# A prologue, a first chunk and a last step in another order, in a fused attention and feed-forward kernel on one core

## The chip, the core and the metric

The kernel runs as one program on one core of a Trainium2 chip. The core has five engines, each with its own list of instructions: PE (TensorE, matmuls and transposes into PSUM), DVE (VectorE), ACT (ScalarE), POOL (GpSimd) and SP (SyncE, which here only issues transfers). They meet through semaphores. Weights are loaded into PE by instructions of their own (PEld). PSUM has eight banks of 128 x 512 f32.

The metric is the device time of one execution in microseconds (us). Three runs of the kernel before took 366.59, 364.92 and 367.21 us, with a median of 366.59.

## What is computed

128 sequences of 64 tokens with 128 features (8192 tokens), all in f32:

```
x = x + xattn(ctx, ctx, layernorm(x))            # 16 heads of 8 features
x = x + ffn(layernorm(x))

xattn: k = KEY @ Wk.T + bk ; v = VALUE @ Wv.T + bv ; q = QUERY @ Wq.T + bq
       score[b,h,i,k] = k[b,h,i] . q[b,h,k] / sqrt(8)
       attn = softmax(score, axis=1)             # axis 1: over the heads
       out  = attn * v, heads joined, @ Wo.T + bo
ffn:   h = x; for blk in 0, 1, 2:
           y = qlora_linear(h; 2 blk); y = gelu(layernorm(y) * gamma + beta)
           y = qlora_linear(y; 2 blk + 1); h = y + h
qlora_linear: w = (q / 7.5 - 1) * scale (one for 16 inputs); x @ w.T + bias + (x @ la.T) @ lb.T
```

## The kernel before, in words

**Attention.** The tokens go through in 16 chunks of 512. Chunk c is worked in four parts p = 0 to 3, each of two sequences. For a part, PE computes the scores of 16 heads into one of two score tiles (`scores`, L1356), DVE takes the maximum over the heads (`negmax`, L815), PE adds its negative with two bf16 matmuls (L1495), ACT takes the exponential (`exponentials`, L1108), DVE sums over the heads and inverts (`zsum` L829, `rz` L832), POOL multiplies (`probs`, L518), and PE multiplies with v, laid out in blocks in `v_diag` (L1564). Between these, the queries and keys of chunk c+2 are made: transposes of the context (L1368) and of the normalised input (L1374), projections (L1380 for q, L1386 for k), and the split of each result in two f16 parts (`q_high`, `q_low`, `k_high`, `k_low` on ACT, with a matmul for the remainder between them, L1400 and L1406). The parts are stored to DRAM by SP and gathered back into `q_stack` and `k_stack` in the layout of the scores. v is projected for chunk c+1 (L1393). DVE also takes the moments of the input three chunks ahead (L607).

**Order.** Nothing is scheduled by a tool: each engine's list is the order in which its function calls stand in `prologue`, `chunk(c, par, half)`, `step(t, par)` and `last_steps`. An engine works strictly down its list, so a wait holds up all that stands behind it on the same engine. `chunks` writes out chunks 0, 1 and 12 to 17 one by one and loops over 2 to 11. Work that is done once stands in the chunks under a condition on (c, p).

**Prologue and work done once.** The prologue loads the first inputs and the weights, makes the queries of chunk 0 in two halves (`first_q_part`), and its keys (`first_key_parts`, DVE, L696 and L699). `keep_awake(n)` is n matmuls of the identity whose result nobody reads. The feed-forward weights are made once: `dequantised_weights` (DVE), `low_rank_products` (PE, six matmuls, L1309), `effective_weights` (DVE: w_eff as their sum, and a fold of the mean into the first, L725 to L738), `transpose_layers` (PE, L1320 and L1321), `transposed_layers` (ACT copies them to `lin_t`, L966), and `first_layer_rows` (PE) with `first_layer_seeds` (DVE, L743 to L753), which make two rows that start later accumulations. In before, `low_rank_products` and the first v projection (`project_v(0)`, into the tile `work0`) stand in part (0, 0) of PE, `effective_weights` in part (0, 1) of DVE after rz, `transpose_layers` in (0, 2) and (1, 0), `first_layer_rows` in (1, 1) and the seeds in (1, 2).

**Feed-forward.** From chunk 13 on and after the attention, `step(t, par)` runs the three blocks as a pipeline over chunks: first layer, moments on DVE, the inverse deviation on POOL (`rs`, a power, L565), scaling on ACT (`normalise`, L1187), transposes on PE, gelu on ACT, second layer. `last_steps` finishes chunks 13 to 15 of the third block; chunk 15 is done in halves of 256 tokens. There, `residual_rows` and `last_layer` put the output of one chunk after the other into the same bank 6, and DVE adds it to x (`add_output`, L921, and L944 for the halves), after which SP stores it.

## Time and profile before

| | |
|---|---|
| median of three runs | 366.59 us (364.92 to 367.21) |
| profiled execution | 366.99 us |
| its span, first to last instruction | 365.0 us |
| PE busy | 342.1 us, 94% |
| DVE busy | 329.3 us, 90% |
| ACT busy | 289.4 us, 79% |
| POOL busy | 267.6 us, 73% |
| mean granted clock of TensorE | 0.986 of 2.4 GHz |

The profiled execution took 2.0 us more than its span; that part lies outside of the instructions. A share of busy time is a mean over stages with different limits. Timeline rows give start and duration in us, then engine, line, operation, tile written and tiles read; a time in square brackets is how long the engine stood idle before the row, with what released it. Consecutive instructions of one engine overlap by 0.1 to 0.2 us in these rows, so the distance between two starts is less than a duration.

### The profile page before, as it was taken

How to read it: one execution, taken by the hardware profiler on the slowest of the kernel's cores; microseconds unless marked ns; L12 is line 12 of the kernel's file. 1: busy time of each engine (PE TensorE's matmuls, PEld its weight loads, DVE VectorE, ACT ScalarE, POOL GpSimd, SP SyncE). 2: the span in 40 equal slices, each digit the busy share in tenths (PEclk: the TensorE clock that was granted, in tenths of full speed). 3: DMA queues.
4: the chain of work that ended last, by engine and by line, in shares of the span. 5: the costliest groups of instructions: out<-in, count | busy, mean ns of one | idle time of the engine just before them, and what ended most of it. 6: DMA issues, size and time to landing. Idle time of an engine off the chain costs nothing.

```text
span 365.0 us, 13072 instructions
## 1 busy us (share of the span) xinstructions
PE 342.1 (94%) x4797; PEld 255.7 (70%) x4797; DVE 329.3 (90%) x816; ACT 289.4 (79%) x587; POOL 267.6 (73%) x287
## 2 busy tenths in 40 slices
PE   6778999999999999999999798988999999999985
PEld 5454666667667667766766576865888888888874
DVE  5798999999999999999999989979999999988762
ACT  4567888888788878878887757668889999999973
POOL 4456688789878877987897998878877788774231
PEclk9889999999999999999999989999999999999999
DMA  7794566576458547645843400000010001101112
GB/s 196 204 284 131 181 203 200 147 237 199 146 172 251 166 135 224 202 155 160 259 137 128 145 2 4 2 1 3 14 47 29 29 29 41 48 30 31 57 31 87
DMA packets 54514, 43.29 MB, mean 119 GB/s; under 512 B 4608, under 2 KB 48592, under 8 KB 54480
## 3 DMA queue, kind: packets, MB, share of 16 engines
q1 hardware_dynamic: 53904, 42.31, 38.5%
q10 hardware_dynamic: 576, 0.53, 0.5%
q8 instruction: 21, 0.34, 0.4%
q14 instruction: 13, 0.11, 0.1%
HBM read 26.05 MB, written 16.78 MB: 117 GB/s over the span
## 4 chain that ended last, share of the span: by engine, by line
PE 64%; DVE 17%; POOL 6%; ACT 6%; issue 5%; DMA 1%; DVEq 0%; ACTq 0%; POOLq 0%
PE score_ps L1594 9%; PE att_ps L1564 6%; PE score_ps L1495 6%; PE wo_ps L1344 5%; DVE zsum L829 4%; PE score_ps L1356 4%; DVE negmax L815 4%; PE score_ps L1687 3%; PE work L1680 3%; PE work L1380 3%; POOL probs L518 3%; PE work L1393 3%; PE work L1386 3%; PE att_ps L1687 3%; PE score_ps L1588 2%
## 5 line engine op out<-in xcount | busy, mean ns | idle before, releaser
L518 POOL TENSOR_TENSOR probs<-probs,rz 128x1024 f32<-128x1024 f32 x64 | 136.3, 2139 | 33.6 <-DVE rz L832 33.5
L565 POOL TENSOR_TENSOR rs<-ve,minus_half 128x4 f32<-128x4 f32 (+1 forms) x48 | 56.6, 1181 | 37.9 <-DVE ve L765 28.4
L829 DVE TENSOR_REDUCE zsum<-probs 128x64 f32<-128x1024 f32 x64 | 77.3, 1209 | 2.2 <-ACT probs L1108 2.0
L815 DVE TENSOR_REDUCE negmax<-score_ps 128x64 bf16<-128x1024 f32 x64 | 75.4, 1180 | 2.0 <-PE score_ps L1356 2.0
L1108 ACT ACTIVATE probs<-score_ps 128x1024 f32<-128x1024 f32 x64 | 65.6, 1025 | 14.2 <-PE score_ps L1495 13.7
L1344 PEld LDWEIGHTS wo_ps<-wo_t,att_t 128*128 128x128 f32 x256 | 37.0, 192 | 13.6 <-issue 12.2
L1564 PE MATMUL att_ps<-probs,v_diag 128*32 128x64 f32 x2048 | 43.8, 225 | 1.3 <-POOL probs L518 1.3
L1594 PEld LDWEIGHTS score_ps<-lin_t,h 128*128 128x128 f32 x304 | 36.9, 191 | 11.1 <-DVE h L914 7.0
L1187 ACT ACTIVATE z<-score_ps,rs 128x128 f32<-128x128 f32 x152 | 43.5, 382 | 0.3 <-POOL rs L565 0.3
L1495 PE MATMUL score_ps<-negmax,ident_bf 128*128 128x512 bf16 x128 | 39.1, 387 | 3.0 <-DVE negmax L815 3.0
L1594 PE MATMUL score_ps<-lin_t,h 128*128 128x128 f32 x304 | 39.7, 278 | 1.8 <-DVE h L914 1.8
L1564 PEld LDWEIGHTS att_ps<-probs,v_diag 128*32 128x32 f32 x2048 | 33.1, 109 | 11.0 <-issue 2.4
L1344 PE MATMUL wo_ps<-wo_t,att_t 128*128 128x128 f32 x256 | 38.1, 275 | 0.0
L832 DVE RECIPROCAL rz<-zsum 128x64 f32<-128x64 f32 x64 | 35.4, 553 | 2.2
L861 DVE BATCH_NORM_STATS2 st<-score_ps 128x6 f32<-128x128 f32 x152 | 33.8, 285 | 3.3 <-PE score_ps L1594 2.2
L1356 PE MATMUL score_ps<-q_stack,k_stack 64*64 64x128 f16 x1024 | 26.8, 223 | 1.5 <-DMA k_stack<-k_parts 0.6
L1356 PEld LDWEIGHTS score_ps<-q_stack,k_stack 64*64 64x64 f16 x1024 | 16.8, 106 | 13.1 <-issue 11.1
L468 POOL TENSOR_TENSOR half_rstd<-veps,minus_half 128x4 f32<-128x4 f32 x16 | 16.3, 1017 | 11.4 <-DVE veps L619 10.4
L1027 ACT ACTIVATE v_diag<-work 64x512 f32<-64x512 f32 x32 | 18.8, 586 | 2.9 <-PE work L1393 2.6
L975 ACT ACTIVATE xln<-x_all,half_rstd 128x128 f32 (+1 forms) x60 | 19.1, 392 | 0.5 <-POOL half_rstd L468 0.5
L1393 PEld LDWEIGHTS work<-w_t_v,ctx_tr 128*128 128x128 f32 x128 | 17.6, 199 | 2.2
L1198 ACT ACTIVATE g<-score_ps,cols 128x512 f32<-128x512 f32 x21 | 16.8, 799 | 2.7 <-PE score_ps L1588 2.7
(234 smaller groups left out, 687.4 us busy)
## 6 DMA issues: line engine op xcount, KB each, us to landing
q_parts<-parts SPq DMA_DIRECT2D x15, 512.0 KB, 3.5
k_stack<-k_parts SPq DMA_DIRECT2D x30, 256.0 KB, 3.3
q_stack<-q_parts SPq DMA_DIRECT2D x60, 128.0 KB, 3.0
ctx_sb<-in_ctx SPq DMA_DIRECT2D x16, 256.0 KB, 3.7
k_parts<-parts SPq DMA_DIRECT2D x16, 256.0 KB, 2.8
out<-x_all SPq DMA_DIRECT2D x15, 256.0 KB, 2.3
x_all<-in_x SPq DMA_DIRECT2D x14, 256.0 KB, 3.9
x_all<-in_x SPq DMA_DIRECT2D x1, 512.0 KB, 5.5
```

What stands on the lines that cost most here:

```text
L518: nc.gpsimd.tensor_tensor(e[:, :, :, :], e[:, :, :, :], by_query.broadcast_to([P, BANDS, SEQ, ADJ]), ALU.mult).then_inc(s_probs, 1)
L565: nc.gpsimd.tensor_tensor(rs2[v][:, lo:hi], ve2[v][:, lo:hi], minus_half[:, lo:hi], ALU.pow).then_inc(p_rs[v], 1)
L815: nc.vector.tensor_reduce(negmax[p % 2][:, :], score_ps[p % 2][:, :].rearrange("p (h k) -> p k h", k=SEQ), AX_X, ALU.max, negate=True).the ...
L829: nc.vector.tensor_reduce(zsum[q][:, :], probs[(p - 1) % 4][:, :, :, :].rearrange("p u k s -> p k u s"), AX_XY, ALU.add).then_inc(s_zsum, 1)
L832: nc.vector.reciprocal(rz[(p - 1) % 4][:, :], zsum[q][:, :]).then_inc(s_rz, 1)
L1108: nc.scalar.activation(probs[p][:, :, :, :], score_ps[p % 2][:, :].rearrange("p (u s k) -> p u k s", s=ADJ, k=SEQ), ACT.Exp, scale=SCALE). ...
L1187: ins = nc.scalar.activation(z[v][0][:, t, :], src[:, TILE * t:TILE * (t + 1)], ACT.Copy, scale=rs2[v][:, lo + t:lo + t + 1])
L1344: ins = nc.tensor.matmul(wo_ps[:, TILE * t:TILE * (t + 1)], att[:, o, TILE * u:TILE * (u + 1)], wo_t[:, o, b, :], start=False, stop=o == 1 ...
L1356: ins = nc.tensor.matmul(score_ps[mp % 2][SEQ * b:SEQ * (b + 1), c0:c0 + 2 * SEQ], k_stack[mb][half_rows, grp, k0:k0 + SEQ], q_stack[mb][h ...
L1495: ins = nc.tensor.matmul(score_ps[p % 2][:, CHUNK * o:CHUNK * (o + 1)], ident_bf[:, :], negmax[p % 2][:, :].unsqueeze(1).broadcast_to([P, ...
L1564: ins = nc.tensor.matmul(att_ps[32 * grp:32 * (grp + 1), c0:c0 + SEQ], v_diag[mb][:, v0:v0 + 32], probs[mp][:, band(hd), :, hd % ADJ], sta ...
L1594: ins = nc.tensor.matmul(dst[:, TILE * t:TILE * (t + 1)], hk[:, TILE * t:TILE * (t + 1)], lin_t[:, 2 * v - 2, :], start=v == 1 and t == 0, ...
```

## The change

Three places are edited.

**The prologue and chunks 0 and 1.** SP loads chunk 2 of x ahead of the weights, the context of chunk 2 ahead of the first stores, and chunk 3 of x alone after the first gathers (before, chunks 2 and 3 came in one transfer after the weights). DVE takes the moments of chunk 1 before the first key parts and those of chunk 2 right behind them. POOL clears the second q_stack before the inverse deviation of chunk 1. PE gets three more `keep_awake` matmuls, `low_rank_products` in two parts in the prologue, and ACT another order of the same copies. In the chunks, v of chunk 0 goes to `wo_ps` instead of `work0` and is projected before the shift of part 0; the transposed layers get two banks, and come in (0, 1) and (0, 2) instead of (0, 2) and (1, 0); the rows come in (0, 3) and the seeds in (1, 0); `effective_weights` stands ahead of zsum in (0, 1). ACT copies the value blocks in (0, 1) instead of (0, 0), and the transposed layers between the high and the low parts.

**The last steps.** Chunk 15's first layer of the third block uses banks 1 and 7, seeded early; its moments, powers and scalings are done by halves, the second scaling by DVE; outputs 14 and 15 have banks of their own (0, 4 and 2) instead of bank 6 in turn.

```diff
@@ sync, prologue
+                sp.dma_start(x_all[:, 2, :, :], x_t[2]).then_inc(s_xin[2], 16)
                 for k, src in (("v", wv), ("o", wo)):
...
-                sp.dma_start(x_all[:, 2:4, :, :], x_pt[:, 2:4, :, :]).then_inc(s_xin[2], 16)
+                sp.wait_ge(s_ctx_ps, 1)
+                sp.dma_start(ctx_sb[0][:, :, :], ctx_t[2]).then_inc(s_ctxin[0], 16)
...
                 gather_first_q(1, s_stack[0])
-                sp.wait_ge(s_ctx_ps, 1)
-                sp.dma_start(ctx_sb[0][:, :, :], ctx_t[2]).then_inc(s_ctxin[0], 16)
+                sp.dma_start(x_all[:, 3, :, :], x_t[3]).then_inc(s_xin[3], 16)
@@ gpsimd, prologue
+                clear(q_stack[1][:, :, :, :].bitcast(F32).rearrange("p g s t -> p (g s t)"), s_const)
                 first_scale(1)
-                clear(q_stack[1][:, :, :, :].bitcast(F32).rearrange("p g s t -> p (g s t)"), s_const)
@@ vector, prologue and chunk
                 bias_columns()
+                next_input(1)
                 first_key_parts()
-                next_input(1)
+                next_input(2)
                 output_weights()
+                low_rank_rows()
                 bias_parts()
-                low_rank_rows()
                 dequantised_weights()
-                next_input(2)
+                last_effective_weights()
...
+                        else:
+                            dve.wait_ge(s_xin[3], 16)
                         dve.wait_ge(s_rstd, c + 3)
                         input_stats_of(c + 3)
+                    if isinstance(c, int) and (c, p) == (0, 1):
+                        effective_weights()
...
-                    if isinstance(c, int) and (c, p) == (0, 1):
-                        effective_weights()
-                    if isinstance(c, int) and (c, p) == (1, 2):
+                    if isinstance(c, int) and (c, p) == (1, 0):
                         first_layer_seeds()
@@ scalar, chunk 0
                     q_high(c + 2, par)
+                    if isinstance(c, int) and c == 0:
+                        transposed_layers(0)
                     q_low(c + 2, par)
+                if isinstance(c, int) and c == 0:
+                    act.wait_ge(s_v_ps, 1)
+                    act.wait_ge(s_vzero, 2)
+                    value_blocks(0, 0, wo_ps)
@@ tensor, prologue
                 transpose_context(0)
+                keep_awake(1)
                 pe.wait_ge(s_wq, 3)
                 nc.tensor.transpose(bank[0][:, 0:P], wq_c[:, :], ident[:, :]).then_inc(s_tr, 1)
+                keep_awake(2)
                 first_transposes(0, wo_ps, h_xln, h_xln_ps)
...
                 project_k(1, 1)
+                low_rank_products(0)
                 project_q(1)
                 k_remainder(1, 1)
+                low_rank_products(1)
                 q_remainder(1, 1)
@@ vector, last steps
                 for u in range(2):
+                    st, ag = st2[3][:, 2 * u:2 * u + 2, :], ag2[3][:, :, 2 * u:2 * u + 2]
                     dve.wait_ge(l_y3, u + 1)
...
+                add_output(13, bank[6])
+                dve.wait_ge(l_rs, 2)
+                dve.wait_ge(l_zt[2], 2)
+                for i in range(2):
+                    ins = nc.vector.tensor_scalar(z[2][0][:, 2 + i, :], last_first_layer(1)[:, TILE * i:TILE * (i + 1)],
+                                                  rs2[3][:, 2 + i:3 + i], None, ALU.mult)
+                ins.then_inc(l_zh, 1)
+                add_output(14, bank[0])
```

The lists show it at three places. First PE, from the scores of parts 0 and 1 on. `work` stands for the tiles work0 and work1, `q_stack` and `score_ps` for both of their buffers. Before:

```order
L1356 MATMUL score_ps<-q_stack,k_stack 64x128 [waits s_lbt,h_stack,h_k_stack]
L1356 MATMUL score_ps<-q_stack,k_stack 64x128 x31
L1495 MATMUL score_ps<-negmax,ident_bf 128x512 [waits s_negmax]
L1495 MATMUL score_ps<-negmax,ident_bf 128x512
L1309 MATMUL att_ps<-la_in,lb_t 128x128 [waits h_q_lo,s_wready,s_lbt]
L1309 MATMUL att_ps<-la_in,lb_t 128x128 x3
L1309 MATMUL wo_ps<-la_in,lb_t 128x128 x2
L1328 MATMUL work<-bias_h,pick_row 128x512 [waits s_q_lo,s_split,s_pick]
L1393 MATMUL work<-w_t_v,ctx_tr 128x128 x4
L1368 MATMUL work<-ident,ctx_sb 128x2x64 [waits s_k_lo,s_ctxin0]
L1368 MATMUL work<-ident,ctx_sb 128x2x64 x3
L1374 MATMUL work<-ident,xln 128x128 [waits s_v,s_xln]
```

And now:

```order
L1391 MATMUL score_ps<-q_stack,k_stack 64x128 [waits h_stack,h_k_stack]
L1391 MATMUL score_ps<-q_stack,k_stack 64x128 x15
L1391 MATMUL score_ps<-q_stack,k_stack 64x128 [waits s_wready]
L1391 MATMUL score_ps<-q_stack,k_stack 64x128 x15
L1363 MATMUL wo_ps<-bias_h,pick_row 128x512 [waits s_split,s_pick,s_weff]
L1428 MATMUL wo_ps<-w_t_v,ctx_tr 128x128 x4
L1541 MATMUL score_ps<-negmax,ident_bf 128x512 [waits s_negmax]
L1541 MATMUL score_ps<-negmax,ident_bf 128x512
L1403 MATMUL work<-ident,ctx_sb 128x2x64 [waits s_k_lo,s_ctxin0]
L1403 MATMUL work<-ident,ctx_sb 128x2x64 x3
L1409 MATMUL work<-ident,xln 128x128 [waits s_q_lo,s_xln]
```

The v projection moved ahead of the shift and into another tile, the low-rank products left this place, and the transposes of the next input no longer wait for the value blocks (s_v).

Second DVE, from the third reciprocal `rz` of chunk 0 to the maximum of part (1, 1). Now:

```order
L829 TENSOR_REDUCE negmax<-score_ps 128x64 [waits s_shifted,s_scores]
L847 TENSOR_REDUCE zsum<-probs 128x64 [waits s_exp]
L850 RECIPROCAL rz<-zsum 128x64 [waits s_zsum]
L756 TENSOR_SCALAR res_cols<-cols 128x1
L757 TENSOR_TENSOR res_cols<-cols 128x1
L761 TENSOR_REDUCE seed_sum<-wo_ps 128x2 [waits s_seed_ps]
L763 TENSOR_SCALAR seed_mean<-seed_sum 128x2 [waits s_seed]
L766 TENSOR_SCALAR seed<-wo_ps,seed_mean 128x128 [waits s_seed]
L766 TENSOR_SCALAR seed<-wo_ps,seed_mean 128x128
L829 TENSOR_REDUCE negmax<-score_ps 128x64 [waits s_shifted,s_scores]
```

The six instructions of the seeds stood six parts' operations later, behind the reciprocal of part (1, 1); they are now right behind that of part (0, 3).

Third ACT at the end. Before:

```order
L1240 ACTIVATE g<-score_ps,cols 128x512 [waits p_c3,p_zt3]
L1267 ACTIVATE z_0<-score_ps,rs_3 128x128 [waits p_rs3]
L1267 ACTIVATE z_0<-score_ps,rs_3 128x128 x3
L1240 ACTIVATE g<-score_ps,cols 128x256 [waits l_zt3,p_c3]
L1240 ACTIVATE g<-att_ps,cols 128x256 [waits l_zt3]
```

And now:

```order
L1297 ACTIVATE z_0<-score_ps,rs_3 128x128 [waits l_rs]
L1297 ACTIVATE z_0<-score_ps,rs_3 128x128
L1274 ACTIVATE g<-score_ps,cols 128x512 [waits p_c3,p_zt3]
L1274 ACTIVATE g<-score_ps,cols 128x256 [waits l_zt3,p_c3]
L1274 ACTIVATE g<-wo_ps,cols 128x256 [waits l_zt3]
```

Two of the four scalings of chunk 15 moved ahead of the gelu of chunk 14, and two left ACT.

## Rows read from the trace of the kernel before

**Rows 1.** Waits of 50 to 190 us: us in total, times, longest us.
```profile
DVE zsum L829 <- ACT probs L1108: 0.4, 2, 0.2
```

**Rows 2.** Chain of waits: start, us, what.
```profile
16.09 4.71 DMA k_stack<-k_parts
...
21.14 0.44 PE score_ps L1356 x16
```

**Rows 3.** Windows: length, busy us of PE, PEld, DVE, ACT, POOL, granted clock, DMA share, GB/s.
```profile
8.20:11.50 3.30, 3.30 (x7) 1.62 (x7) 0.75 (x1) 1.27 (x6) 0.00 (x0) 0.50 1.17 248
```

**Rows 4.** Timeline of PE: the same key projection at either clock.
```profile
8.08 2.07 PE L1386 MATMUL work<-ctx_tr,w_t_k 128*128 128x512 f32 x2
...
17.42 1.12 PE L1386 MATMUL work<-ctx_tr,w_t_k 128*128 128x512 f32 x2 [0.16 <-ACT ctx_tr L983]
```

**Rows 5.** Timeline of DVE in the prologue.
```profile
11.80 0.75 DVE L699 TENSOR_SCALAR parts<-work,cols_h 128x512 f16<-128x512 f32 x1 [0.78 <-PE work L1406]
12.47 0.86 DVE L607 BATCH_NORM_STATS2 stats<-x_all 128x6 f32<-128x128 f32 x4
```

**Rows 6.** Timeline of SP's queue: key store, query gathers.
```profile
13.05 0.61 SPq L363 DMA_DIRECT2D k_parts<-parts  x1
...
15.49 3.91 SPq L391 DMA_DIRECT2D q_stack<-q_parts  x8
```

**Rows 7.** Timeline of DVE in chunks 0 and 1.
```profile
21.61 2.36 DVE L815 TENSOR_REDUCE negmax<-score_ps 128x64 bf16<-128x1024 f32 x2 [0.71 <-PE score_ps L1356]
...
26.91 0.41 DVE L727 TENSOR_TENSOR w_eff<-wo_ps,w_deq 128x256 f32<-128x256 f32 x1
...
27.55 1.13 DVE L733 TENSOR_TENSOR fold<-cols,fold 128x1 f32<-128x1 f32 x1
...
29.55 1.22 DVE L815 TENSOR_REDUCE negmax<-score_ps 128x64 bf16<-128x1024 f32 x1 [0.36 <-PE score_ps L1356]
31.13 1.22 DVE L829 TENSOR_REDUCE zsum<-probs 128x64 f32<-128x1024 f32 x1 [0.35 <-ACT probs L1108]
...
36.11 1.23 DVE L815 TENSOR_REDUCE negmax<-score_ps 128x64 bf16<-128x1024 f32 x1 [0.20 <-PE score_ps L1356]
37.87 1.22 DVE L829 TENSOR_REDUCE zsum<-probs 128x64 f32<-128x1024 f32 x1 [0.53 <-ACT probs L1108]
...
39.59 1.16 DVE L815 TENSOR_REDUCE negmax<-score_ps 128x64 bf16<-128x1024 f32 x1
...
45.94 0.10 DVE L743 TENSOR_SCALAR res_cols<-cols 128x1 f32<-128x1 f32 x1
```

**Rows 8.** Timeline of POOL beside it.
```profile
26.53 2.13 POOL L518 TENSOR_TENSOR probs<-probs,rz 128x1024 f32<-128x1024 f32 x1 [2.67 <-DVE rz L832]
...
29.88 1.01 POOL L468 TENSOR_TENSOR half_rstd<-veps,minus_half 128x4 f32<-128x4 f32 x1
```

**Rows 9.** Timeline of DVE: two casts, before and after POOL began to clear.
```profile
14.98 0.22 DVE L663 CAST bias<-row_r 16x128 bf16<-16x128 f32 x1
...
15.22 0.52 DVE L664 CAST row_mid<-row_r 16x128 bf16<-16x128 f32 x1
```

**Rows 10.** Timeline of POOL beside them.
```profile
15.12 2.10 POOL L494 MEMSET q_stack<- 128x512 f32 x4
```

**Rows 11.** Timeline of ACT in the last steps.
```profile
356.86 0.78 ACT L1240 ACTIVATE g<-score_ps,cols 128x512 f32<-128x512 f32 x1 [1.30 <-PE score_ps L1588]
358.57 1.14 ACT L1267 ACTIVATE z<-score_ps,rs 128x128 f32<-128x128 f32 x4 [0.93 <-POOL rs L565]
360.39 0.56 ACT L1240 ACTIVATE g<-score_ps,cols 128x256 f32<-128x256 f32 x1 [0.68 <-PE score_ps L1694]
```

**Rows 12.** Timeline of PE in the last steps.
```profile
357.69 1.16 PE L1705 MATMUL work<-lin_t,g 128*128 128x128 f32 x8 [0.43 <-ACT g L1240]
```

**Rows 13.** Timeline of DVE: the last addition.
```profile
362.21 0.42 DVE L944 TENSOR_TENSOR x_all<-score_ps,x_all 128x256 f32<-128x256 f32 x1
```

**Rows 14.** The page, DMA issues: count, KB each, median us to landing.
```profile
x_all<-in_x SPq DMA_DIRECT2D x14, 256.0 KB, 3.9
```

More of the change, by code:

```diff
@@ L195, in build @@
         s_seed = sem("s_seed")
-        s_xin = [sem(f"s_xin{i}") for i in range(3)]
+        s_xin = [sem(f"s_xin{i}") for i in range(4)]
         s_xnext = [sem(f"s_xnext{i}") for i in range(2)]
@@ L309, in turned_bank, with last_first_layer @@
         def turned_bank(i):
[L311 removed]
+            return (att_ps if i < 4 else wo_ps)[:, P * (i % 4):P * (i % 4 + 1)]
+        def last_first_layer(u):
+            return (bank[1], bank[7])[u][:, 0:2 * TILE]
         def half_tiles(u):
@@ L598, in _ @@
             steps(pool, step)
-            for t in (20, 21):
-                step(t, t % 2)
+            step(20, 0)
+            pool.wait_ge(p_z[3], 15)
+            for u in range(2):
+                pool.wait_ge(l_st, u + 1)
+                nc.gpsimd.tensor_tensor(rs2[3][:, 2 * u:2 * u + 2], ve2[3][:, 2 * u:2 * u + 2],
+                                        minus_half[:, 2 * u:2 * u + 2], ALU.pow).then_inc(l_rs, 1)
         @block.vector
@@ L1093, in prologue @@
                 q_low(1, 1)
-                transposed("v", bank[5], 4)
-                act.wait_ge(s_tr, 5)
-                nc.scalar.activation(wo_t[:, :, :, :].rearrange("p o b n -> p (o b n)"), bank[4],
-                                     ACT.Copy).then_inc(s_wready, 1)
                 nc.scalar.activation(neg_last[:, :], cols[:, ROW_BL + 5:ROW_BL + 6].broadcast_to([P, P]), ACT.Copy,
@@ L1254, in last_steps @@
                 gelu(3, g[2][:, :], bank[3])
-                act.wait_ge(p_z[2], 16)
-                half_seed(0)
                 normalise(3, 14, 0, 15, bank[0])
-                act.wait_ge(p_z[3], 15)
-                half_seed(1)
+                act.wait_ge(l_rs, 1)
+                for t in range(2):
+                    ins = nc.scalar.activation(z[2][0][:, t, :], last_first_layer(0)[:, TILE * t:TILE * (t + 1)], ACT.Copy,
+                                               scale=rs2[3][:, t:t + 1])
+                ins.then_inc(l_z[3], 1)
                 act.wait_ge(p_zt[3], 15)
@@ L1263, in last_steps @@
                 gelu(3, g[2][:, :], bank[3])
-                act.wait_ge(p_rs[3], 16)
-                for t in range(TPC):
-                    u = t // 2
-                    ins = nc.scalar.activation(z[3][0][:, t, :], bank[1 - u][:, TILE * t:TILE * (t + 1)], ACT.Copy,
-                                               scale=rs2[3][:, t:t + 1])
-                    if t == 1:
-                        ins.then_inc(l_z[3], 1)
-                ins.then_inc(p_z[3], 1)
                 act.wait_ge(p_c[3], 15)
@@ L1275, in last_steps @@
                     act.wait_ge(l_zt[3], u + 1)
-                    gelu(3, g[2][:, half_columns(u)], bank[(3, 4)[u]][:, half_columns(u)])
+                    gelu(3, g[2][:, half_columns(u)], bank[(3, 5)[u]][:, half_columns(u)])
             prologue()
@@ L1517, in chunk @@
                         project_q(c + 2)
+                    if isinstance(c, int) and (c, p) == (0, 1):
+                        transpose_layers(0)
                     if p == 2 and live(c + 2):
@@ L1707, in last_layer @@
                     return ins
+                pe.wait_ge(p_h[0], 16)
+                nc.tensor.matmul(last_first_layer(1), ident_bf[:, :], pick_row[:, 0:2, :], start=True,
+                                 stop=True).then_inc(l_open, 1)
                 pe.wait_ge(p_h[2], 15)
```

165 lines of the change are left out of this document (89 added, 76 removed).

## The prediction

> **What bounds the kernel now.** I read the busy shares first: PE 94% and DVE 90% both look like the bound, so shares don't decide. The waits of the steady loop do. Between 50 and 190 us DVE waited 0.4 us in all [rows 1]: there it is the bound, with PE close behind, and nothing in this change touches the loop. So a lead that DVE has when it enters the loop is a lead at the end of the loop, and a microsecond that PE alone wins is worth nothing. What is left is the start, up to about 47 us, and the last 15 us.
>
> At the start the chain of waits runs through the first gathers of the keys: the second one is issued at 16.09, lands 4.71 later, and the scores begin at 21.14 [rows 2]. Ahead of it TensorE works at half its clock: granted 0.50 (1.2 GHz) from 8.2 to 11.5 us, after a stretch with three gaps of 0.4 to 0.5 us in which it waited for a context, a weight and an input [rows 3]. The same key projection takes 2.07 us there and 1.12 us at the full clock [rows 4]. Behind the first scores I read DVE's timeline: from its first maximum to the fourth reciprocal it has five stretches in which it does no work of its own [rows 7].
>
> **The prologue.** The three added keep_awake matmuls fill 0.2 and 0.45 us of those gaps and end before the wait behind them is over, so they delay nothing. I take it that the clock then stays up. That is worth at least 0.95 us (the projection alone, 2.07 - 1.12) and at most 1.65 us (half of 3.3 us at half clock [rows 3]). Step by step: the projection starts at 8.08 as now and ends at 9.2, the first key part takes 0.75 (as L699 [rows 5]), the remainder 0.45, so the second key part starts at 10.4 instead of 11.80 [rows 5]: 1.4 us. The moments of chunk 1, at 12.47 now [rows 5], go into the time in which DVE waits for the key projection, and the inverse deviation of chunk 1 is no longer what the scalings and, behind them on ACT, the key gathers stand in line for. The key store then goes out at 11.7 (now 13.05), and the query gathers at 13.7 (now 15.49 [rows 6]), since the two stores between them come off a shorter chain. The gathers' bytes are the same, so I let the 4.7 us of [rows 2] run from 1.4 to 1.8 us earlier: scores at 19.5 instead of 21.14, **1.65 us**. What is added there is hidden: the low-rank products on PE stand in the wait for the gathers (the last matmul of the prologue ends near 18.4 by the same steps); the last effective weights on DVE end near 19.4, just before the first maximum at 19.95. That margin of 0.5 us is thin, and I charge nothing for it.
>
> **Chunk 0.** From 21.61 to 39.59 DVE takes 17.98 us for four maxima pairs, one set of moments, the effective weights and four sums with reciprocals [rows 7]. Of these, 0.36 + 0.35 + 0.20 + 0.53 = 1.44 us are waits for PE and ACT. Another 0.97 us is one instruction, the fold on one column: 1.13 us where its like takes 0.16. It ends at 28.68, and POOL's multiplication, 26.53 + 2.13, at 28.66 [rows 7, 8]: a DVE instruction with two inputs in SBUF is held until POOL's is over. In the new order it runs near 23.8, when POOL has nothing to do before the first reciprocal (26.4), so this goes. A third piece, 0.32 us of L727 [rows 7], moves to the prologue. Do the waits go? PE's list up to the scores of part 2 loses the low-rank products and the wait for the value blocks: these scores come at 23.0 (DVE wants them at 26.3), those of part 3 at 26.0 (wanted 29.2), part (1, 0) at 30.2 (wanted 32.0), the third exponential ends at 29.2 (wanted 30.3). The least slack is 0.8 us, so DVE works without a gap. 1.44 + 0.97 + 0.32 = **2.73 us**. Below it would be 1.3 (no wait goes), above nothing.
>
> **The seeds.** They are moved, so their 1.3 us of work costs the same. But their place is new: right behind the reciprocal of part 3, at 35.2. POOL is late there: multiplication 0 ends at 28.6, the variance of the input, which ends with the power at 29.88 + 1.01 [rows 8], holds it until 30.9, and multiplications 1, 2 and 3 follow without a gap until 33.0, 35.15 and 37.3. L757 of the new list is the same operation with the same form as the fold, two inputs in SBUF, one column. If it or the seed mean behind it is held until multiplication 3 ends, DVE loses 2.1 us; if both pass in the handover at 35.15, nothing. For the mean, with one input, the rows are further off: a cast took 0.22 us just before POOL began to clear at 15.12 and 0.52 us after it [rows 9, 10], so one input from SBUF to SBUF can be held too. I take **2.0 us lost**, by the fold, which is nearest.
>
> The Trainium skill (SBUF — State Buffer, Who interferes with whom) says that VectorE and GpSimd share a pair of ports with an exclusive lock, taken by a VectorE instruction with two SBUF inputs while GpSimd reads, and by a tensor_scalar that gets into a two-port mode. By it the seed mean is held even if L757 slips through, which speaks against this change; the loss would be 2.0 us in either order. The row of the fold agrees with the first half; no row of before shows the second for a tensor_scalar.
>
> Start of the loop: 1.65 + 2.73 - 2.0 = **2.4 us** earlier on DVE, and kept to the end of the loop.
>
> **The last steps.** Now the gelu of chunk 14 ends at 357.64, its last layer at 358.85, and from then on the buffer g is free for the halves of chunk 15, yet their gelu starts at 360.39: 1.54 us [rows 11, 12]. In between stand four scalings (1.14 us, behind the gelu), the addition that frees bank 6, and two transposes. With half of the scalings ahead of the gelu, the other half on DVE and banks of their own, nothing is left in this gap but the semaphore, 0.04. The first two scalings (0.6 us) fall in the 1.30 us in which ACT waits for this gelu's input [rows 11], but come late in it, and one opening matmul is added on PE: together the gelu starts 0.2 later. **1.3 us**; the second half's power and DVE's scaling end near 358.0, 0.7 before they are wanted, so the new wait hides. Bounds: 0 (the halves' chain just replaces the old one) to 1.5. From the gelu's start to the last addition, 360.39 to 362.63 [rows 11, 13], all stays.
>
> **Sum.** 366.99 - 2.4 - 1.3 = 363.3 us for the profiled execution. It stood 0.4 above the median, so I forecast **362.9 us**.
>
> **Rivals.**
> - *The seeds are not held.* For it: the loss hangs on POOL's being three multiplications behind, and the handover at 35.15 lies 0.05 us from where the seeds start. Against it: the fold. Time 360.9.
> - *The clock falls all the same,* or falls in another place as costly. For it: the gap before the context, 0.5 us, stays, and the granted clock fell a second time, at 25 us, after a busier stretch. Then the 1.65 us are not won: 364.5.
> - *The end gives nothing:* 364.2. For it: six waits among four engines are new there. Against it: each is early by my times.
> - *Slower, by the load of chunk 3.* DVE now waits for it at 22.3 before the effective weights, the first sum and the first reciprocal, with PE's transposed layers and the scores of part 3 queued behind. It goes out at 17.5, after eight gathers, and such a load takes 3.9 us [rows 14], so it lands at 21.4, with 0.9 to spare. Every microsecond after 22.3 costs one; from 26.0 on the kernel is slower than before, and at 27.0 it takes 367.6. Nothing in the profile shows a load of 9.5 us.
>
> **Chances.** The forecast 0.48, the seeds not held 0.24, the clock 0.15, nothing at the end 0.09, the load 0.04. 1% is 3.7 us, about what a measurement of this kernel can tell from no change: below 362.9 counts as faster. My forecast lies on that line; a little over half of it I give to faster. With the seeds not held, all of it is faster; the next two are within 1%. So faster 0.51, within 1% 0.45, slower 0.04. The range of 360.7 to 365.0 takes in the first four cases with their own spread and leaves out what lies below the second and the slow one.
>
> **What would show it.** The granted clock from 8 to 11.5 us at 1.00 and the key projection at 1.1 us; the first scores near 19.5; the fold at 0.16 us near 24; DVE without waits from its first maximum to the fourth reciprocal; L757 or L763 lasting 1 to 2 us, ending with a POOL multiplication; DVE 2.4 us ahead when it is in the loop (the maximum that stood at 47.2 after the seeds); no gap between the last layer of chunk 14 and the gelu of chunk 15. I am wrong if DVE waits for the scores or exponentials of chunk 0, or if its lead shrinks inside the loop, which would mean that PE or a transfer is the bound there.

## The result: 0.9% faster, and the profile after

The changed kernel takes 362.09 us (median of 15 runs, 361.35 to 363.73), the one before 365.87 us (15 runs, 362.86 to 368.21). The ratio is 0.9914, 95% interval 0.9886 to 0.9941 (the two medians alone give 0.990). Ratios in this text leave out runs more than 1.5% above the fastest of their kernel; medians keep them. The forecast was 362.9 us. The profiled execution of the change took 362.27 us with a span of 360.4, against 366.99 and 365.0 before: 4.6 us of span, where the sum had 3.7.

The first thing that differs is TensorE's clock. The page of the profile shows it in slices of 9 us, each digit the granted clock in tenths; before and after:

```profile
PEclk9889999999999999999999989999999999999999
```

```profile
PEclk9999899999999999999999999999999999999999
```

Before, the granted clock fell at 8, at 25 and at 209 us; after, once, at 39 us, and neither at 8 nor at 25. The windows of after show the stretch of [rows 3], then the two microseconds before the fall, and the fall itself (columns as there):

```profile
8.20:11.50 3.30, 2.76 (x11) 1.39 (x10) 2.11 (x8) 2.33 (x9) 3.12 (x7) 1.00 1.09 220
36.90:39.00 2.10, 0.13 (x9) 0.07 (x2) 2.06 (x6) 0.35 (x1) 0.18 (x1) 1.00 0.68 221
39.30:42.70 3.40, 3.40 (x37) 1.44 (x35) 3.37 (x6) 1.71 (x2) 1.26 (x1) 0.51 0.03 8
```

Between 36.9 and 39.0 TensorE worked for 0.13 us in all. DVE's timeline says what it waited for. These rows answer to [rows 7]:

```profile
19.87 2.35 DVE L829 TENSOR_REDUCE negmax<-score_ps 128x64 bf16<-128x1024 f32 x2
...
23.95 0.16 DVE L746 TENSOR_TENSOR fold<-cols,fold 128x1 f32<-128x1 f32 x1
...
26.25 1.16 DVE L829 TENSOR_REDUCE negmax<-score_ps 128x64 bf16<-128x1024 f32 x1
...
31.82 1.16 DVE L829 TENSOR_REDUCE negmax<-score_ps 128x64 bf16<-128x1024 f32 x1
...
34.14 0.55 DVE L850 RECIPROCAL rz<-zsum 128x64 f32<-128x64 f32 x1
34.61 0.10 DVE L756 TENSOR_SCALAR res_cols<-cols 128x1 f32<-128x1 f32 x1
34.62 0.37 DVE L757 TENSOR_TENSOR res_cols<-cols 128x1 f32<-128x1 f32 x1
34.91 0.41 DVE L761 TENSOR_REDUCE seed_sum<-wo_ps 128x2 f32<-128x256 f32 x1
35.35 1.75 DVE L763 TENSOR_SCALAR seed_mean<-seed_sum 128x2 f32<-128x2 f32 x1
37.14 0.61 DVE L766 TENSOR_SCALAR seed<-wo_ps,seed_mean 128x128 f32<-128x128 f32 x2
37.66 1.21 DVE L829 TENSOR_REDUCE negmax<-score_ps 128x64 bf16<-128x1024 f32 x1
```

From the first maximum to that of part (1, 0) no row has an idle time in brackets. The fold takes 0.16 us where it took 1.13. Then the seed mean takes 1.75 us where it took 0.17 in its old place. POOL beside it, and the matmul that waits for the late maximum:

```profile
30.74 6.33 POOL L524 TENSOR_TENSOR probs<-probs,rz 128x1024 f32<-128x1024 f32 x3
```

```profile
38.94 0.81 PE L1541 MATMUL score_ps<-negmax,ident_bf 128*128 128x512 bf16 x2 [1.97 <-DVE negmax L829]
```

POOL's three multiplications end at 37.07, the seed mean at 37.10. TensorE waits 1.97 us for the next maximum.

At the end ACT shows the other part of the change; the rows answer to [rows 11]:

```profile
353.50 0.78 ACT L1274 ACTIVATE g<-score_ps,cols 128x512 f32<-128x512 f32 x1
355.81 0.56 ACT L1274 ACTIVATE g<-score_ps,cols 128x256 f32<-128x256 f32 x1 [1.53 <-PE score_ps L1737]
```

From the gelu of chunk 14 (ends 354.28) to the first of chunk 15 there are now 1.53 us; before there were 2.75 (357.64 to 360.39).

How far DVE is at the same maxima, from its timelines, in us. Two more executions stand beside the two: one of either kernel in which the clock never fell (the runs "before again" and "after again" below), and the changed kernel with its seeds in the old place.

| DVE is at | before | after | before, clock up | after, clock up | seeds back |
|---|---|---|---|---|---|
| maximum (0, 0) | 21.61 | 19.87 | 19.87 | 20.13 | 19.77 |
| maximum (1, 0) | 36.11 | 31.82 | 33.47 | 32.08 | 31.71 |
| maximum (1, 1) | 39.59 | 37.66 | 36.95 | 37.93 | 34.50 |
| maximum (1, 3) | 47.20 | 44.06 | 44.55 | 44.33 | 42.11 |
| maximum (3, 0) | 62.51 | 59.93 | 59.85 | 59.57 | 57.41 |
| maximum (5, 2) | 93.94 | 91.73 | 91.33 | 91.41 | 88.84 |
| maximum (13, 2) | 195.19 | 193.03 | 192.58 | 192.73 | 190.15 |
| maximum (15, 0) | 216.51 | 213.13 | 212.66 | 212.84 | 210.23 |
| last addition | 362.21 | 357.63 | 358.30 | 357.41 | 354.74 |

The first two columns are the pair that was forecast: 1.74 us ahead at the first maximum, 4.29 at (1, 0), 3.14 behind the seeds, 2.16 in the loop, 3.38 behind the fall at 209, 4.58 at the end. The third and fifth are what the rest of this text is about: with the clock up, the first maximum of the kernel before stands at 19.87 too.

### The profile page after: what moved, and what is told of

Same layout as the page of the kernel before. It is cut to its first block, busy times and chain, and to the rows that moved or that the text cites. A ratio compares the mean times of both kernels' runs of the same rounds, so it can differ in the third digit from the quotient of the medians.

```text
span 360.4 us, 13093 instructions
## 1 busy us (share of the span) xinstructions
PE 340.1 (94%) x4804; PEld 254.6 (71%) x4804; DVE 331.7 (92%) x821; ACT 288.2 (80%) x585; POOL 266.8 (74%) x288
## 4 chain that ended last, share of the span: by engine, by line
PE 62%; DVE 23%; POOL 5%; issue 5%; ACT 3%; DVEq 0%; POOLq 0%; ACTq 0%
PE score_ps L1637 9%; PE att_ps L1600 7%; DVE zsum L847 6%; PE score_ps L1541 5%; DVE negmax L829 5%; PE wo_ps L1379 5%; PE score_ps L1391 3%; PE score_ps L1730 3%; PE work L1723 3%; PE work L1415 3%; POOL probs L524 3%; PE att_ps L1730 3%; PE score_ps L1631 2%; PE work L1428 2%; PE work L1421 2%
## 5 line engine op out<-in xcount | busy, mean ns | idle before, releaser
L524 POOL TENSOR_TENSOR probs<-probs,rz 128x1024 f32<-128x1024 f32 x64 | 136.2, 2141 | 37.0 <-DVE rz L850 36.9
L571 POOL TENSOR_TENSOR rs<-ve,minus_half 128x4 f32<-128x4 f32 (+1 forms) x47 | 55.6, 1184 | 34.3 <-DVE ve L778 24.7
L1379 PEld LDWEIGHTS wo_ps<-wo_t,att_t 128*128 128x128 f32 x256 | 36.9, 191 | 13.4 <-issue 12.0
L1637 PEld LDWEIGHTS score_ps<-lin_t,h 128*128 128x128 f32 x304 | 36.9, 191 | 11.1 <-DVE h L930 7.0
L1723 PEld LDWEIGHTS work<-lin_t,g 128*128 128x128 f32 x104 | 13.7, 192 | 6.2 <-issue 6.2
L1058 ACT ACTIVATE v_diag<-work 64x512 f32<-64x512 f32 x30 | 17.6, 585 | 0.3
```

Of the source, the lines that this page charges most:

```text
L524: nc.gpsimd.tensor_tensor(e[:, :, :, :], e[:, :, :, :], by_query.broadcast_to([P, BANDS, SEQ, ADJ]), ALU.mult).then_inc(s_probs, 1)
L571: nc.gpsimd.tensor_tensor(rs2[v][:, lo:hi], ve2[v][:, lo:hi], minus_half[:, lo:hi], ALU.pow).then_inc(p_rs[v], 1)
L1379: ins = nc.tensor.matmul(wo_ps[:, TILE * t:TILE * (t + 1)], att[:, o, TILE * u:TILE * (u + 1)], wo_t[:, o, b, :], start=False, stop=o == 1 ...
L1637: ins = nc.tensor.matmul(dst[:, TILE * t:TILE * (t + 1)], hk[:, TILE * t:TILE * (t + 1)], lin_t[:, 2 * v - 2, :], start=v == 1 and t == 0, ...
```

## Experiments

There were four series, each on another chip and beside its own runs of the kernel before: experiments 1 to 4, 5 to 7, 8 to 11, and 12. The ratio is to these runs. One more run of the kernel before, in the first series, took 836.88 us at a mean clock of 1.0; it is left out everywhere. "Clock up" counts the runs whose mean granted clock was 0.998 or more; every fall of some 3.5 us takes 0.005 off that mean. Of the kernel before 4 of 33, 0 of 11, 2 of 16 and 1 of 11 runs kept the clock up in the four series, so counts from different series are compared with care.

| kernel | runs | median us | ratio, 95% | clock up | their median | mean clock |
|---|---|---|---|---|---|---|
| before, beside the experiments | 71 | 365.78 | | 7 | 363.31 | 0.990 |
| after | 15 | 362.09 | 0.9914 (0.9886 to 0.9941) | 7 | 361.49 | 0.9955 |
| keep_awake only | 12 | 366.34 | 1.0013 (0.9976 to 1.0050) | 3 | 363.73 | 0.989 |
| after, no keep_awake | 12 | 362.83 | 0.9936 (0.9906 to 0.9965) | 4 | 362.09 | 0.994 |
| start only | 12 | 363.76 | 0.9941 (0.9914 to 0.9968) | 6 | 363.51 | 0.9965 |
| end only | 11 | 363.93 | 0.9945 (0.9908 to 0.9983) | 2 | 361.92 | 0.992 |
| seeds back | 6 | 360.28 | 0.9842 (0.9796 to 0.9887) | 5 | 359.95 | 0.998 |
| no mean | 6 | 360.00 | 0.9841 (0.9794 to 0.9888) | 5 | 359.86 | 0.9985 |
| seeds and fold back | 11 | 363.60 | 0.9919 (0.9887 to 0.9951) | 0 | | 0.9885 |
| seeds back, no keep_awake | 6 | 361.30 | 0.9871 (0.9832 to 0.9911) | 0 | | 0.993 |
| seeds back, no mean | 6 | 359.17 | 0.9814 (0.9776 to 0.9852) | 6 | 359.18 | 0.9997 |
| the same, rank later | 6 | 360.23 | 0.9853 (0.9805 to 0.9901) | 3 | 359.63 | 0.995 |

### 1. The three matmuls alone

```diff
                 transpose_context(0)
+                keep_awake(1)
                 pe.wait_ge(s_wq, 3)
...
+                keep_awake(2)
                 first_transposes(0, wo_ps, h_xln, h_xln_ps)
```

> The kernel before with nothing but the three added keep_awake matmuls. Theory (the clock's fall at 8.2 us comes from TensorE's gaps before it, and the time to the scores hangs on the key projection): granted clock 1.00 from 8 to 11.5 us, key projection 1.1 instead of 2.07, first maximum at 20.0 to 20.7 instead of 21.61, time 0.9 to 1.6 us below the kernel before. Rival (the matmuls are too few, or the scores wait for the deviation and the gathers of chunk 1's neighbours, not for the projection): clock 0.5 there again or the first maximum within 0.3 of 21.61, time within 0.4 us.

The profile has the clock up from 8 to 11.5 us and the first maximum at 20.31, 1.3 us earlier than in the profile of before: that half of the theory holds. The time does not follow: 366.34 us, no difference that can be measured. The profiled execution is one of the long ones, because the clock fell later instead:

```profile
22.80:36.50 13.70, 12.40 (x72) 8.31 (x71) 9.31 (x17) 6.31 (x9) 6.19 (x8) 0.50 0.39 125
```

13.7 us at the lower level, and DVE 2.9 us behind the profile of before at (1, 1). Five of the 12 runs had a mean clock of 0.984 or less, against 7 of 33 of the kernel before in that series. So filling the first gaps kept the clock up at 8 us in this profile, and did not keep later falls away while chunk 0 is as before.

### 2. The change without them

```diff
                 transpose_context(0)
-                keep_awake(1)
...
-                keep_awake(2)
                 first_transposes(0, wo_ps, h_xln, h_xln_ps)
```

> The changed kernel without the three added keep_awake matmuls. Theory: the clock falls at 8 us again, the key projection takes 2 us, the first maximum comes 0.9 to 1.7 us later than 19.87, and the time rises by the same, to 0.9 to 1.7 above the changed kernel. Rival (the new order alone has closed the gaps): the clock stays up without them, the first maximum at 19.9, no difference over 0.3 us.

The clock fell at 8 us in the profile, and the first maximum stands at 21.09, 1.22 later than 19.87. But the median rises by 0.7 only, and 4 of 12 runs kept the clock up. These 0.7 us are not clear of noise (the two intervals overlap, and the runs come from different series), and with the clock up the two still differ by 0.6 (362.09 against 361.49), so how much of it is falls is not shown. Part of the lost lead came back further on: that profile had no fall at 39 us, and at (3, 0) it is 0.6 behind the changed kernel.

### 3 and 4. The start alone, the end alone

Start only is the changed kernel with the last steps as before; end only the reverse. In DVE's list of the latter:

```diff
-                add_output(13)
 
                 for u in range(2):
+                    st, ag = st2[3][:, 2 * u:2 * u + 2, :], ag2[3][:, :, 2 * u:2 * u + 2]
                     dve.wait_ge(l_y3, u + 1)
...
+                add_output(13, bank[6])
+                dve.wait_ge(l_rs, 2)
+                dve.wait_ge(l_zt[2], 2)
```

> The changed kernel with the last steps of the kernel before. Theory (the two halves of the change add up, and the end gives the 1.2 us by which ACT's gap before the last gelus shrank): 1.2 us above the changed kernel, gelu gap 2.75 us again. Rival (the end was shortened by an earlier arrival of work that is off the path): under 0.5 us above.

> The kernel before with the last steps of the changed kernel. Theory: 1.2 us below the kernel before, gap on ACT between the gelu of chunk 14 and the first of chunk 15 1.5 us instead of 2.75; nothing changes ahead of 340 us, and the three falls of the granted clock stay where they were. Rival: under 0.5 us below.

Taking the end away costs 1.7 us (363.76 against 362.09, from different series), giving it alone wins 1.6 (363.93 against 365.54 in that series). The profiles put it in one gap on ACT. Start only, and end only:

```profile
357.43 0.56 ACT L1253 ACTIVATE g<-score_ps,cols 128x256 f32<-128x256 f32 x1 [0.67 <-PE score_ps L1719]
```

```profile
355.49 0.78 ACT L1265 ACTIVATE g<-score_ps,cols 128x512 f32<-128x512 f32 x1
357.79 0.56 ACT L1265 ACTIVATE g<-score_ps,cols 128x256 f32<-128x256 f32 x1 [1.53 <-PE score_ps L1716]
```

The second has the gap of 1.53 us again. So the end is worth 1.2 us of gap, and 0.4 more in the medians, which the profiles don't place.

One part of the expectation missed, and it opened the case: end only has the prologue of before, word for word, yet its first maximum stands at 20.13 and the clock did not fall at 8. Falls belong to the run, not to the kernel alone. And of the start, with the clock up, hardly anything is left: 363.51 us against 363.31 for the kernel before.

### 5 to 7. The seeds, and the kernel before once more

Seeds back:

```diff
-                    if isinstance(c, int) and (c, p) == (1, 0):
+                    if isinstance(c, int) and (c, p) == (1, 2):
                         first_layer_seeds()
```

No mean (the seeds stay at (1, 0)):

```diff
-                nc.vector.tensor_scalar(seed_mean[:, :], seed_sum[:, :], -1.0 / D, None, ALU.mult).then_inc(s_seed, 1)
-                dve.wait_ge(s_seed, 3)
                 for v in range(2):
-                    ins = nc.vector.tensor_scalar(seed[:, v, :], raw[:, v, :], seed_mean[:, v:v + 1], None, ALU.add)
+                    ins = nc.vector.scalar_tensor_tensor(seed[:, v, :], seed_sum[:, v:v + 1].broadcast_to([P, P]),
+                                                         -1.0 / D, raw[:, v, :], ALU.mult, ALU.add)
```

> The changed kernel with the first layer's seeds back in their old place, behind part (1, 2). Theory (the seeds were held in the new place until POOL's multiplications ended, which starved TensorE for 2 us and brought the clock down at 39 us): the seed mean takes 0.17 us instead of 1.75, the maximum of part (1, 1) stands near 35.3 instead of 37.66, that of part (1, 3) near 42.4 instead of 44.06, no gap of 2 us on PE near 37 and no fall of the clock at 39; time 0.8 to 1.6 us below the changed kernel. Rival (TensorE is the next bound, so DVE's lead is taken back in the first chunks of the loop): the same at part (1, 3), but DVE waits for exponentials from then on and the time is within 0.5 us of the changed kernel.

> The changed kernel with the seeds in their new place, but the seed mean (tensor_scalar from SBUF to SBUF) taken out: the sum goes straight into a scalar_tensor_tensor that reads one operand in SBUF and one in PSUM. Theory (it is this instruction's form that is held by POOL): no instruction of the seeds lasts over 0.7 us, maximum of part (1, 1) near 35.9 instead of 37.66. Rival (whatever follows the reciprocal there is held): the hold of 1.6 us moves to the next instruction and part (1, 1) stays near 37.6. Time: as with the seeds in the old place, within 0.4 us, by the first; as the changed kernel by the second.

> The kernel before once more, for one profile in which the granted clock may fall less often than in the first (33 runs of it spread from 363.1 to 369.4 us with their mean clock between 1.0 and 0.981). With fewer falls the first maximum should stand near 20.1 (as in the run with only the end changed) instead of 21.61.

Both are 1.8 to 2.1 us below the changed kernel, a little more than the 0.8 to 1.6 that I had expected. Seeds back:

```profile
34.50 1.16 DVE L829 TENSOR_REDUCE negmax<-score_ps 128x64 bf16<-128x1024 f32 x1
...
41.38 0.17 DVE L763 TENSOR_SCALAR seed_mean<-seed_sum 128x2 f32<-128x2 f32 x1
```

No mean, with POOL beside it:

```profile
35.12 0.38 DVE L757 TENSOR_TENSOR res_cols<-cols 128x1 f32<-128x1 f32 x1
35.42 0.41 DVE L761 TENSOR_REDUCE seed_sum<-wo_ps 128x2 f32<-128x256 f32 x1
35.87 0.48 DVE L764 SCALAR_TENSOR_TENSOR seed<-seed_sum,wo_ps 128x128 f32<-128x128 f32 x2
36.27 1.22 DVE L828 TENSOR_REDUCE negmax<-score_ps 128x64 bf16<-128x1024 f32 x1
```

```profile
31.25 6.34 POOL L524 TENSOR_TENSOR probs<-probs,rz 128x1024 f32<-128x1024 f32 x3
```

POOL multiplies until 37.59, and four instructions of DVE pass beside it: one operand in SBUF and one in PSUM is not held, nor is a reduction. L757, with both in SBUF, is held for 0.23 us, up to the handover between two multiplications. So the first theory of each holds: it is the seed mean, a `tensor_scalar` of 128x2 from SBUF to SBUF, that was held for 1.58 us. One input from SBUF to SBUF is not enough for a hold. The rows of the changed kernel above have two such instructions beside the same multiplications, and neither is held: the reciprocal at 34.14 (0.55 us, as everywhere else) and L756 at 34.61, a `tensor_scalar` of one column (0.10 us). The rival of seeds back (the lead is taken back in the loop) falls: DVE is 2.45 us ahead of "before, clock up" at (1, 1) and 2.43 at (15, 0), and both runs kept the clock up.

Before again came out at 362.98 us with a mean clock of 1.0, and is the third column of the table above. Its rows:

```profile
19.87 2.36 DVE L815 TENSOR_REDUCE negmax<-score_ps 128x64 bf16<-128x1024 f32 x2
...
26.06 1.13 DVE L733 TENSOR_TENSOR fold<-cols,fold 128x1 f32<-128x1 f32 x1
...
35.22 1.22 DVE L829 TENSOR_REDUCE zsum<-probs 128x64 f32<-128x1024 f32 x1 [0.53 <-ACT probs L1108]
```

The held fold and the wait of 0.53 us are there with the clock up as well; the waits of 0.36 and 0.35 of [rows 7] are gone. TensorE's gaps ahead of 8 us were not the same in the two executions either. Before, and before again:

```profile
5.66 0.66 PE L1368 MATMUL work<-ident,ctx_sb 128*128 128x128 f32 x4 [0.47 <-DMA ctx_sb<-in_ctx]
6.72 0.33 PE L1442 MATMUL score_ps<-ident,wq_c 128*128 128x128 f32 x1 [0.41 <-DVE wq_c L629]
7.49 0.44 PE L1418 MATMUL wo_ps<-ident,xln 128*128 128x128 f32 x2 [0.44 <-ACT xln L1049]
```

```profile
5.89 1.11 PE L1368 MATMUL work<-ident,ctx_sb 128*128 128x128 f32 x4 [0.37 <-DMA ctx_sb<-in_ctx]
6.97 0.33 PE L1442 MATMUL score_ps<-ident,wq_c 128*128 128x128 f32 x1
7.49 0.44 PE L1418 MATMUL wo_ps<-ident,xln 128*128 128x128 f32 x2 [0.18 <-ACT xln L1049]
```

The four transposes of the context take 0.66 us in one and 1.11 in the other, both at a granted clock of 1.00, and the longer ones leave two short gaps where there were three. Why they take longer is open.

### 8 to 11. The fold back, the matmuls out, both mendings, and the change once more

Seeds and fold back (on top of seeds back):

```diff
-                    if isinstance(c, int) and (c, p) == (0, 1):
-                        effective_weights()
                     mc = c - (p == 0)
...
+                    if isinstance(c, int) and (c, p) == (0, 1):
+                        effective_weights()
                     if isinstance(c, int) and (c, p) == (1, 2):
```

The next is seeds back with the edit of experiment 2, then seeds back with the edit of no mean.

> The changed kernel with the seeds in their old place (as in the fifth run) and the effective weights behind the first reciprocal again, where POOL's first multiplication runs. Theory (a DVE instruction with two inputs in SBUF is held until POOL's multiplication ends): the fold takes 1.1 us instead of 0.16 and ends with it, DVE reaches part (1, 0) 0.9 to 1.4 us later than 31.71, and the time is 0.8 to 1.6 us above the run with the seeds in their old place (360.3). Rival (only the first reciprocal's place matters, POOL has slack): under 0.4 us.

> The changed kernel with the seeds in their old place and without the three added keep_awake matmuls. Theory (they only lower the chance of the clock's fall at 8 us, which costs 1.2 us when it comes): some runs as fast as 359.4 to 360.3 at a clock of 1.0, others 1.0 to 1.5 us longer at 0.995, median 0.3 to 1.2 us above 360.3. Rival (without the starved stretch behind the seeds the clock holds anyway): no difference over 0.3 us.

> Both mendings of the changed kernel together: seeds in their old place and the seed mean folded into the subtraction. By either theory there is no hold left to take away, so only the 0.2 us of the mean itself can be won: 360.0 to 360.3, fastest of all by nothing that can be measured. If it were held in the old place too, it would be below 359.5.

> The changed kernel once more, for a profile without a fall of the clock (7 of its 15 runs had none). Against the undisturbed profile of the kernel before it should be even at the first maximum (19.87), 2.35 us ahead before the seeds, 0.5 to 0.7 ahead behind them, the same at 190 us, and 1.8 at the end (span 359.3 to 359.6).

The fold in its old place is held again, DVE and POOL:

```profile
30.06 1.32 DVE L746 TENSOR_TENSOR fold<-cols,fold 128x1 f32<-128x1 f32 x1
```

```profile
29.24 2.12 POOL L524 TENSOR_TENSOR probs<-probs,rz 128x1024 f32<-128x1024 f32 x1 [6.79 <-DVE rz L848]
```

It ends at 31.38, the multiplication at 31.36. Median 3.3 us above seeds back, twice what the theory allowed, and not one of 11 runs kept the clock up (with the fold in its new place 5 of 6 runs of seeds back did, and 6 of 6 of "seeds back, no mean" in the series of this one). The fastest run, 361.90 with one fall, is 2.5 above the fastest of seeds back. The profile is no clean measure of the rest: a weight landed late there (TensorE waited 1.94 us for wq_c) and the first maximum stands at 24.33.

Without keep_awake the median is 1.0 above, as expected, though the two intervals overlap and the series differ. It comes by another way: all six runs have a fall, and the one of the profile stands at 205 us, with the first maximum at 19.84. The theory (a fall at 8) missed its place.

Both mendings: 359.17 us, with the clock up in all six runs. It is the fastest version, 1.9% below the kernel before (0.9776 to 0.9852). I had expected 360.0 to 360.3, and a time below 359.5 if the mean were held in the old place too. It is below, but the mean was not held there: it took 0.17 us in the profile of seeds back. The profile of this version spans 357.3 us, that of seeds back 357.5, and DVE goes from maximum (1, 2) to (1, 3), past the seeds, in 3.72 us instead of 4.05. So the mean's share is 0.2 to 0.3 us. The two ran in different series, and the rest of the 1.1 us between the medians stays open.

After again is the fourth column above. I expected 0.5 to 0.7 us of lead behind the seeds and found 0.22, and from (5, 2) on none. The last addition is 0.89 earlier than in before again (358.30 to 357.41), where I had expected 1.8, and the span is 360.2 us, not 359.3 to 359.6. The first maximum was 0.26 late in this run, and 0.3 us went between (4, 3) and (5, 0). That second loss, 0.2 to 0.4, is in all five profiles with the seeds at (1, 0); with them at (1, 2) it is 0.1 at most. Between 50 and 190 us DVE waits 1.0 us for exponentials in the changed kernel, in four waits, against 0.6 in three in seeds back; why a delay 40 us earlier leaves that is open.

### 12. The low-rank products

```diff
-                low_rank_products(1)
                 q_remainder(1, 1)
...
                 scores(0, 0)
+                low_rank_products(1)
```

with the addition of the last effective weights behind the first maximum on DVE, on top of both mendings.

> The tenth run's kernel (both mendings) with the second pair of low-rank products behind the scores of part (0, 0) on TensorE, and its addition on DVE behind the first maximum. Theory (in the undisturbed prologue TensorE works without a gap from 14.3 us to the scores, so 0.7 us of low-rank products stand on the path; the query gathers land 0.3 to 0.4 earlier than before): scores 0.2 to 0.6 us earlier than 19.18, the addition's 0.32 us goes back into DVE's chunk 0, so part (1, 1) stands within 0.3 us of 34.5 and the time within 0.4 us of the tenth run (359.2). Rival (the gathers are the bound of the scores): scores at 19.1 to 19.4 as now, part (1, 1) 0.3 us later.

```profile
17.85 0.38 PE L1441 MATMUL work<-parts,neg_ident 128*128 128x512 f16 x1
18.79 0.39 PE L1435 MATMUL work<-parts,neg_ident 128*128 128x512 f16 x1 [0.56 <-ACT parts L1031]
19.18 0.42 PE L1391 MATMUL score_ps<-q_stack,k_stack 64*64 64x128 f16 x16
```

The scores start at 19.18, just as with seeds back. The 0.7 us of products were not on TensorE's path: without them it waits 0.56 us for ACT's part of chunk 1's queries, whose remainder stands ahead of the scores in its list. So my theory fell. The rival's two numbers came (scores at 19.1 to 19.4, maximum (1, 1) at 34.75 against 34.50), but in this execution it is ACT and not a gather that the scores stand behind. In others it is the gathers of the keys, as in start only:

```profile
19.77 0.64 PE L1373 MATMUL score_ps<-q_stack,k_stack 64*64 64x128 f16 x32 [0.59 <-DMA k_stack<-k_parts]
```

After again (0.48 us, scores at 19.66) and no mean (0.60, at 19.89) wait for them too. So in the new order it is now ACT's part of the queries and now the key gathers that come last, and the scores start between 19.18 and 19.89. On DVE the addition of the last effective weights did stand in the way a little: with it behind the first maximum, that maximum comes at 19.64 instead of 19.77.

The time missed: 360.23 us in the median, 1.1 above the version without this edit, where I had allowed 0.4. Three of the six runs kept the clock up, against six of six. The profiled run, with no fall, took 359.17 us, the same as that version's median.

## Why the prediction was right, step by step

**The bound: right.** DVE's lead at the start of the loop arrives at its end. Seeds back against "before, clock up", 2.45 and 2.43 us, shows it best. In the pair that was forecast the lead went from 3.14 to 2.16, which I had named as a sign of being wrong. Half of it went between (2, 3) and (3, 0), only in the two profiles whose clock had fallen at 39 us; 0.3 is the loss between (4, 3) and (5, 0).

**The prologue: the number right, the value not.** 1.65 us was forecast, 1.74 measured, with the key projection at 1.13 us and the query gathers at 13.93 instead of 15.49. All of it is the clock. With the clock up the old order has its first maximum at 19.87 as well, and the new one stands at 19.64 to 20.36 in all its profiles without an early fall. The query gathers go out 0.34 us earlier (13.93 against 14.27), but the forecast's chain ran through the key gathers, and these go out no earlier: the first at 14.55 and 14.21 in the two profiles of the changed kernel, at 14.23 in before again. Beside them TensorE's list is done at 19.2, not at 18.4 as I had worked out, by experiment 12 for ACT's part of chunk 1's queries. DVE had no margin of 0.5 us either: its last effective weights (L735) ended at 19.89, not at 19.4. The sum held because the profile of before was an execution with three falls, which is luck. 7 of 71 runs have none. The rival "the clock falls all the same", 364.5 us, was put as a yes or no for the kernel; it is a share of the runs.

**Chunk 0: right.** Forecast 2.73. Measured 2.55 up to (1, 0), and the 0.53 us wait behind it: 3.1. With the clock up the old order has less to lose (waits 0.53, fold 0.97, L727 0.32, and two short stretches of 0.23 each without a releaser): 2.35 us, 17.08 against 14.73 from (0, 0) to (1, 1) with seeds back. (The stretch holds five maxima, not four pairs as I wrote; the sum doesn't hang on it.)

**The seeds: size right, reason half right.** 2.0 us forecast, 1.8 measured (1.58 at the mean, 0.22 at L757). I had put it on L757, by its likeness to the fold. L757 was let through at 34.96, in the handover between two multiplications. What was held is the seed mean. The Trainium skill (SBUF — State Buffer, Who interferes with whom) says that `tensor_scalar` can take the shared ports and then waits for GpSimd's whole instruction, while a reduction never contends and an instruction with one SBUF input outside these modes doesn't either. The traces agree in each: 1.75 us for L763 and 0.41 for L761 in the changed kernel, 0.48 for the two of L764 in no mean, all while POOL multiplied. The rival "not held" (360.9) thus was wrong for this kernel, and its time, made real by seeds back and no mean, came to 360.3 and 360.0.

What the step left out is who waits for DVE there: TensorE was idle for 2.0 us, and the clock fell behind it in two of the four profiles that have the hold.

**The end: right.** 1.3 us forecast, 1.22 measured as the shorter gap, 1.6 and 1.7 in the medians of experiments 3 and 4. The load of chunk 3, my slower case, went out at 18.17, and its moments began at 22.14 without a wait.

**What was not in the sum:** the fall at 209 us, 1.2 us of DVE's time in before and none in after. It is luck of the two executions. "Before, clock up" has the same waits at that place (0.79 us for a maximum, then 1.33 for POOL) and no fall.

So the 3.7 us of the sum and the 3.8 of the medians agree, but they are not made of the same parts. With the clock up in both, the change is worth 1.8 us in the medians (363.31 to 361.49). Some 1.2 of that is the end. For the start the terms leave 0.55 (chunk 0's 2.35 less the seeds' 1.8) and nothing for the prologue, and even the 0.55 is not shown: start only with the clock up takes 363.51 us against 363.31, and in the two profiles with the clock up the changed kernel is 0.22 us ahead behind the seeds and 0.18 behind at (15, 0). The other 2 us of the medians go with falls that come less often (mean clock 0.990 to 0.9955). I got the whole right by taking one execution with three falls as the base and forecasting one without.

**Open:** what decides whether the clock falls in a run. At 8 us the gaps themselves differ between two executions of the same list (experiment 7). But at 39 us the same wait of TensorE (1.97 and 1.95 us) was followed by a fall in after and by none in after again. The waits between 202 and 213 us are the same in all profiles, and the clock fell behind them in three of 14. So the gaps alone don't decide it. Two things went with fewer falls, each only with the other, in runs of different series: the matmuls in the gaps (none of six runs up without them, five of six with) and a chunk 0 without the held fold (none of 11, five of six).

## What to carry to other kernels

A stretch at half clock in the one profile that is at hand is a fact about that run. Look at the mean clock of all runs before giving an edit the whole of what the stretch costs, and compare runs with the same clock.

When work moves on DVE, ask what POOL is doing at that moment, and then look at the form. Here a `tensor_scalar` of 128x2 and a cast, both from SBUF to SBUF, and a `tensor_tensor` with both inputs in SBUF waited until POOL's instruction was over. A reduction, an instruction with an operand in PSUM, a reciprocal and a `tensor_scalar` of one column did not. A place 6 us later, or another form of the same arithmetic, won as much here (1.8 to 2.1 us) as the whole change does with the clock up.

## What the runs showed of the hardware

The same program on the same data falls into TensorE's lower clock level a different number of times: 71 runs of the kernel before lie between 363.07 us at a mean clock of 1.0 and 369.41 at 0.984. Those at 0.993 to 0.995, about one fall, are 1.5 us longer than those with none (in the changed kernel 0.8). Between 202 and 213 us all 14 profiles have the same two waits of TensorE, 0.8 and 1.33 us. In end only the clock fell behind them, in before again it didn't:

```profile
208.15 1.08 PE L1586 MATMUL att_ps<-probs,v_diag 128*32 128x64 f32 x32 [1.33 <-POOL probs L524]
```

```profile
206.97 0.68 PE L1564 MATMUL att_ps<-probs,v_diag 128*32 128x64 f32 x32 [1.33 <-POOL probs L518]
```

A cast is held by a fill as a `tensor_scalar` is by a multiplication: in the changed kernel's prologue L679 took 1.77 us (to 17.38) and ended with POOL's clearing of v_diag (15.38 + 1.92 = 17.30). The cast L673, at 14.80 and ahead of the clearing, took 0.22:

```profile
15.61 1.77 DVE L679 CAST bias<-row_r 16x128 bf16<-16x128 f32 x1
```

```profile
15.38 1.92 POOL L500 MEMSET v_diag<- 128x512 f32 x4
```
